# The front of an attention block in a written-out order: who evicts a tile's first group, when two query weights are loaded, and in which pieces two heads' second halves are computed

## The chip, the cores and the metric

One Trainium2 chip; the same program runs on 8 cores at once, each on its own 1024 rows (own rows), without talk between the cores. The metric is the device time of the slowest core in microseconds (us), lower is better. Engines: TensorE (PE: matmuls, transposes), VectorE (DVE), ScalarE (ACT), GpSimd (POOL), and SyncE (SP), which issues loads. Each engine works through its own list of instructions in order; where an instruction waits for a semaphore, all that stands behind it on the engine waits too.

## The reference, cut to what matters

x is (2, 4096, 4096) in float32. Two layers: `x = x + LN(attn(LN(x)))`, then `x = x + LN(ffn(LN(x)))`.

```python
Q = (x @ Wq.T).reshape(B, S, 32, 128)        # 32 heads
K = x @ Wk.T; V = x @ Wv.T                   # one head of 128, shared
Qr = Q*cos + rotate_half(Q)*sin; Kr likewise # "rope"
# windows of 512 keys every 256 rows: sigmoid(scores*SCALE), each row divided by
# its sum, then @ V; neighbouring windows are blended linearly
return out @ Wo.T
# ffn: x @ base_W.T + 2 * (gates of the top 2 of 8 experts * (x@A_e)) @ B_e
```

## The kernel before, in words

Each core holds 12 tiles of 128 rows: 8 own tiles and 4 neighbour tiles (halo), of which only K and V are needed. `ORDER` gives the order of loading: positions 0 to 7 are the own tiles, 8 to 11 the halo tiles. The part that changes is the front, up to about 185 us, where x becomes K, V and the first queries. After it come 128 steps of attention (with the other heads' queries between the steps), the Wo projection, the second layer norm with transposes and router, and the base projection.

What happens to a tile i in the front:

- `load_x(i)` on SP: three DMAs (2048, 1024, 1024 columns, 2 MB in all) into one of three buffers `xst`, once tile i-3 is normalised.
- `ln1_stats(i)` on VectorE: eight `bn_stats` (L260), then the aggregate and two small instructions.
- `ln1_apply(i)` on ScalarE: three small instructions, then two activations that write the normalised bf16 tile `xn` by halves (L278).
- `ln1_tr(i, g)` on TensorE, g = 0 to 3: eight 128x128 transposes each (L300) into one PSUM bank. There are three banks, `T1_BANK = [0, 1, 7]`, and group 3 takes group 0's: it waits until group 0 is evicted. Groups 0 and 1 need the first half of `xn`, 2 and 3 the second.
- eviction into `ln1T` (or `halo`): groups 0 to 2 on ScalarE (L309), group 3 on VectorE (`ln1_ev3`, L319).
- `kv_mm(i, 0, 32)` on TensorE: 32 matmuls of 256 columns (L329), after all four evictions. `k_rope(i)` on VectorE (L343 to L348), `k_tr(i)` on TensorE (L353, L355) with a copy on ScalarE (L358).

Queries: a job is half a head, 512 rows wide: 32 matmuls in 8 groups of 4 (`q_group`, L406), into bank 4 or 5. Jobs run (0,0), (1,0), (0,1), (1,1), then (2,0), (2,1), (3,0), (3,1), as (head, half). Half 0 needs tiles 0 to 3, half 1 tiles 4 to 7. `ropes()` queues the rope of each finished job on VectorE: four instructions (L418 to L424), of which the first three read the bank. A head's 1 MB weight (2 MB in DRAM, cast by the DMA) comes by `load_wq` on POOL's queue; heads 0 and 1 use slots 2 and 3, and heads 2 and 3 use the same two after them.

The order: in `start_stage(i)`, TensorE gets groups 0 to 2 of tile i-1, K and V of tile i-2, and group 3 of tile i-1. VectorE gets the eviction of group 3, `k_rope(i-2)` and the statistics of tile i+1. ScalarE gets the evictions and `ln1_apply(i)`. Then come `k_tr(i-3)` and, from stage 4 on, four query groups (eight from stage 8), and ropes from stage 7. Weight 0 is loaded once tile 3's first part has landed, cos and sin after tile 4, weight 1 after tile 5's first part.

In the later stage (about 1206 to 1311 us) a loop over 8 tiles computes slab 0 of the base projection. Ahead of the next tile's transposes (`tr_group`, L874), which wait for VectorE's `st_d` (L862), an `early` call puts eight matmuls of slab 1 as filler at t = 2, 3, 4 and 5. Their weights, pieces 38 and 39, are loaded at t = 0 by POOL's queue, behind its own addition `st_add` (L847).

Of the kernel before, what the change touches and what calls it, by code (L numbers as in the profile page):

```python
# [9 lines left out]
BF16 = mybir.dt.bfloat16  # L10
# [10 lines left out]
NTX = 12  # L21
# [66 lines left out]
def tok(s):  # L88
    return (s, s.n)


def build_program():
# [156 lines left out]
    def load_kcs(i):  # L249
        buf, ext = i % 4, ORDER[i]  # L250
        P.op("sync", lambda e: e.dma_start(out=kcs_s[buf][:, :], in_=kcs[ext * 128:(ext + 1) * 128, :]),
             waits=([krp_tok[i - 4]] if i >= 4 else []), inc=s_kcs[buf], inc_by=16)
        kcs_tok[i] = tok(s_kcs[buf])

    ln1_in = {}

    def ln1_stats(i):
        buf, q = i % 3, i & 1
        for k in range(8):
            P.op("vector", lambda e, k=k: e.bn_stats(st[:, q, k, :], xst[buf][:, 512 * k:512 * (k + 1)]),  # L260
                 waits=([x_part[i][{0: 0, 4: 1, 6: 2}[k]]] if k in (0, 4, 6) else []), inc=(s_f if k == 7 else None))
        P.op("vector", lambda e: e.bn_aggr(mv[q], st[:, q, :, :]),
             waits=[tok(s_f)] + ([xap_tok[i - 2]] if i >= 2 else []), inc=s_f)
        P.op("vector", lambda e: e.tensor_scalar(lnv[q], mv[q][:, 1:2], EPS, None, ALU.add),
             waits=[tok(s_f)], inc=s_f)
        P.op("vector", lambda e: e.tensor_scalar(mv[q][:, 0:1], mv[q][:, 0:1], -1.0, None, ALU.mult), inc=s_f)
        ln1_in[i] = tok(s_f)
# [27 lines left out]
    def ln1_tr(i, g):  # L295
        q, bk = i & 1, g % 3
        pb = ps[T1_BANK[bk]].bitcast(BF16)
        for k in range(8):
            dt = 8 * g + k
            P.op("tensor", lambda e, k=k, dt=dt: e.transpose(  # L300
                    pb[:, k * 128:(k + 1) * 128], xn[q][:, dt * 128:(dt + 1) * 128], identB[:, :]),
                 waits=([xap_half[(i, g // 2)], ID_READY] + t1_free[bk]) if k == 0 else [],
                 inc=(s_t1 if k == 7 else None))
        t1_tok[i] = [tok(s_t1)]
        src = pb.rearrange("p (a b) -> p a b", a=8)
        dst = ln1_view(i)(8 * g, 8 * g + 8)
        halo_free = [kv_tok[i - 2]] if ORDER[i] in (10, 11) and g == 0 else []
        if g < 3:
            P.op("scalar", lambda e: e.activation(out=dst, in_=src, func=AF.Copy),  # L309
                 waits=[tok(s_t1)] + halo_free, inc=s_t1a)  # L310
            t1_free[bk] = [tok(s_t1a)]
            ev_tok.setdefault(i, []).append(tok(s_t1a))

    def ln1_ev3(i):
        pb = ps[T1_BANK[0]].bitcast(BF16)
        src = pb.rearrange("p (a b) -> p a b", a=8)
        dst = ln1_view(i)(24, 32)
        halo_free = [kv_tok[i - 2]] if ORDER[i] in (10, 11) else []
        P.op("vector", lambda e: e.tensor_copy(dst, src), waits=t1_tok[i] + halo_free, inc=s_t1v)  # L319
        t1_free[0] = [tok(s_t1v)]  # L320
        ev_tok[i].append(tok(s_t1v))

    kvb_free = [[], []]

    def kv_mm(i, d0, d1):
        bk = i & 1
        view = ln1_view(i)
        for d in range(d0, d1):
            P.op("tensor", lambda e, d=d: e.matmul(  # L329
                    ps[2 + bk][:, 0:256], view(d, d + 1), wkv_s[:, d, :], start=(d == 0), stop=(d == 31)),  # L330
                 waits=((ev_tok[i] + kvb_free[bk]) if d == 0 else [])
                 + ([WKV_READY[d // 8]] if i == 0 and d % 8 == 0 else []),
                 inc=(s_kv if d == 31 else None))
        if d1 == 32:
            kv_tok[i] = tok(s_kv)
# [132 lines left out]
    load_kcs(0)  # L468
    load_kcs(1)

    def start_stage(i):

        if i >= 1 and i - 1 < NTX:
            for g in range(3):
                ln1_tr(i - 1, g)
        if i >= 2:
            kv_mm(i - 2, 0, 32)
        if i >= 1 and i - 1 < NTX:
            ln1_tr(i - 1, 3)
            ln1_ev3(i - 1)  # L480
        if i >= 2:
            k_rope(i - 2)
            if i + 2 < NTX:
                load_kcs(i + 2)
        if i + 1 < NTX:
            ln1_stats(i + 1)
        if i < NTX:
            ln1_apply(i)
            if i + 3 < NTX:
                load_x(i + 3)  # L490
            if i < 2:
                load_kcs(i + 2)
        if i == 1:
            load_wq(0, [x_part[3][0]])
            P.op("gpsimd", lambda e: e.dma_start(out=cosT_s[:, :], in_=cosT[:, :]),
                 waits=[x_part[4][2]], inc=s_cs, inc_by=16)
            P.op("gpsimd", lambda e: e.dma_start(out=sinS_s[:, :], in_=sinS[:, :]), inc=s_cs, inc_by=16)
            cs_ready.append(tok(s_cs))
        if i == 3:
            load_wq(1, [x_part[5][0]])  # L500
        if i == NTX:
            load_wq(4, t1_tok[NTX - 1])
            load_wq(5, t1_tok[NTX - 1])

    ln1_stats(0)
    Q_AHEAD = 64
    for i in range(NTX + 2):
        start_stage(i)
        if i >= 3 and i - 3 < NTX:
            k_tr(i - 3)  # L510
        if i == NTX:
            use_table(AF.Sigmoid)
        if i >= 4:
            for _ in range(4 if i < 8 else 8):
                if q_pos[0] < Q_AHEAD:
                    q_next()
            if i >= 7:
                ropes()
    for h in wq_late:
        load_wq(h, [wq_done[h - 4]])  # L520
    k_tr(NTX - 1)
    while q_pos[0] < Q_AHEAD:
        q_next()
    ropes()
    KR_READY = tok(s_kev)
    KV_DONE = tok(s_kv)
    V_READY = tok(s_vcp)
# [476 lines left out]
    for t in range(NT):  # L1004
        router_mm(t)
        if t + 1 < NT:
            st_d(t + 1)
        router_chain(t)
        if t + 3 < NT:
            st_n(t + 3)  # L1010
            st_add(t + 3, "gpsimd")
            if t + 5 < NT:
                load_xr(t + 5)
        b = t & 1
        breg = ps[b][:, 0:512]
        proj_mms(breg, ln2T, t, BA_P[0], 0, 16, bank_free[b] + [t2_tok[t]], t == NT - 1, t == 0, False)
        if t == 0:
            w7(16, 32)
            w7_done()
            load_piece(38)  # L1020
            load_piece(39)
        elif 2 <= t < 6:
            early((t - 2) // 2, 16 + 8 * ((t - 2) % 2))
        if t + 1 < NT:
            tr_group(t + 1, 0)
            tr_group(t + 1, 1)
        proj_mms(breg, ln2T, t, BA_P[0], 16, 24, [], t == NT - 1, t == 0, False)
# [181 lines left out]
```

How the kernel before makes its waits and increments, by code:

```python
                    def body(eng):  # L76
                        for fn, waits, inc, inc_by in oplist:
                            for s, v in waits:
                                if v > 0:
                                    eng.wait_ge(s.h, v)
                            inst = fn(eng)
                            if inc is not None:
                                inst.then_inc(inc.h, inc_by)
```

## Time and profile before

| | us |
|---|---|
| three timed runs | 1740.9, 1743.73, 1717.39; median 1740.9 |
| the profiled execution | 1722.67 |
| its span on the slowest core (4) | 1721.1 |
| spans, cores 0 to 7 | 1713.3, 1717.1, 1718.1, 1715.8, 1721.1, 1718.3, 1721.1, 1717.4 |
| granted clock, all cores | 0.986 to 0.991 of full speed |
| TensorE busy, core 4 | 1635.1 (95%) |
| VectorE, ScalarE busy, core 4 | 681.9, 559.1 |

The page is of core 4, the slowest. Busy is the time in which an engine has an instruction at work; a row of the timeline merges neighbouring instructions of one kind, and the bracket gives idle time before it and what ended that. TensorE's matmuls overlap, so the distance from start to start tells a group's cost better than its length.

### The profile page before, as it was taken

Reading aid. Unit: us, or ns where it says so; the run is one execution under the profiler, and the core shown is the slowest. Engines: PE = TensorE matmul, PEld = TensorE weight load, DVE = VectorE, ACT = ScalarE, POOL = GpSimd, SP = SyncE. Lnnn points to the kernel's source line nnn. Section 1 sums busy time; section 2 is a strip of 40 time slices with the busy share of each in tenths; the row PEclk is TensorE's granted clock in tenths of the full one; section 3 lists DMA queues with packets and bytes.
Section 4 is the critical chain, followed back from the end, with each engine's and each line's share of the span. In section 5 each row is a group of like instructions: output and inputs, shape, how many; then the busy total and the mean of one; then the engine's idle time right before and its main releaser. Section 6 shows DMA issues by size and latency. Waiting matters only on the chain.

```text
span 1721.1 us, 29291 instructions; the slowest of 8 cores (1713.3 to 1721.1 us)
## 1 busy us (share of the span) xinstructions
PE 1635.1 (95%) x10425; PEld 933.0 (54%) x10600; DVE 681.9 (40%) x1715; ACT 559.1 (32%) x906; POOL 147.1 (9%) x180
## 2 busy tenths in 40 slices
PE   2779999999999999999999999999899999999996
PEld 2556566666666666654444444458555444444763
DVE  4575466665666666661000100003882011000065
ACT  3755344554544554451000000011442000000154
POOL 0000000000000000000000000002650000000010
PEclk8899999999999999999999999999999999999998
DMA  9972624666666632227663356533746425642689
GB/s 232 272 248 55 113 50 74 99 99 99 106 105 109 112 63 50 50 53 127 98 98 61 53 83 98 83 93 121 228 146 112 73 50 88 101 68 51 133 250 288
DMA packets 33852, 193.37 MB, mean 112 GB/s; under 512 B 4528, under 2 KB 7216, under 8 KB 17200
## 3 DMA queue, kind: packets, MB, share of 16 engines
q0 software_dynamic: 20752, 139.57, 45.2%
q1 hardware_dynamic: 12672, 51.91, 9.3%
q8 instruction: 89, 1.46, 0.4%
q14 instruction: 51, 0.42, 0.1%
q10 hardware_dynamic: 288, 0.01, 0.0%
HBM read 279.66 MB, written 41.94 MB: 187 GB/s over the span
## 4 chain that ended last, share of the span: by engine, by line
PE 89%; DMA 5%; DVE 2%; issue 2%; ACT 1%; POOL 0%; SPq 0%; DVEq 0%; ACTq 0%; POOLq 0%
PE ps_all L712 49%; PE ps_all L406 25%; PE ps_all L570 5%; PE ps_all L547 5%; DMA xst<-x_ext 4%; PE ps_all L329 2%; DMA wslot<-wb_scratch 1%; PE ps_all L616 1%; PE ps_all L936 1%; PE ps_all L300 1%; PE ps_all L890 1%; PE ps_all L874 1%; DVE st L260 0%; POOL proj L847 0%; DVE st L729 0%
## 5 line engine op out<-in xcount | busy, mean ns | idle before, releaser
L406 PE MATMUL ps_all<-ln1T,wslot 128*128 128x512 bf16 x1960 | 453.0, 381 | 12.9 <-DVE ln1T L319 8.4
L712 PE MATMUL ps_all<-wslot,ln2T 128*128 128x512 bf16 (+1 forms) x2256 | 452.2, 356 | 5.7 <-DMA wslot<-wb_scratch 3.2
L712 PE MATMUL ps_all<-wslot,attn_T 128*128 128x512 bf16 (+1 forms) x2266 | 441.7, 355 | 2.6 <-ACT attn_T L621 0.6
L729 DVE BATCH_NORM_STATS2 st<-proj 128x6 f32<-128x512 bf16 x192 | 126.4, 687 | 659.6 <-ACT proj L721 659.6
L712 PEld LDWEIGHTS ps_all<-wslot,attn_T 128*128 128x128 bf16 x2304 | 224.8, 98 | 217.0 <-issue 0.8
L712 PEld LDWEIGHTS ps_all<-wslot,ln2T 128*128 128x128 bf16 x2304 | 224.2, 98 | 216.2 <-issue 4.3
L406 PEld LDWEIGHTS ps_all<-ln1T,wslot 128*128 128x128 bf16 x2048 | 200.2, 98 | 223.5 <-issue 11.7
L721 ACT ACTIVATE proj<-ps_all 128x512 bf16<-128x512 f32 (+1 forms) x144 | 78.5, 548 | 680.8 <-PE ps_all L712 378.5
L556 ACT ACTIVATE sig<-ps_all 128x1536 bf16<-128x1536 f32 x128 | 185.6, 1450 | 3.7 <-PE ps_all L547 3.7
L621 ACT ACTIVATE attn_T<-ps_all 128x256 bf16<-128x256 bf16 x128 | 49.1, 383 | 230.2 <-PE ps_all L616 230.2
L570 PEld LDWEIGHTS ps_all<-v_aug,sig 128*128 128x128 bf16 x1536 | 99.5, 98 | 36.8 <-issue 9.5
L570 PE MATMUL ps_all<-v_aug,sig 128*128 128x129 bf16 (+1 forms) x1536 | 113.1, 221 | 3.1 <-DVE cbl L604 2.1
L600 DVE SCALAR_TENSOR_TENSOR ct<-ps_all,urs,ct 128x128 f32<-128x128 f32 x256 | 88.8, 347 | 48.1 <-ACT ct L595 47.6
L604 DVE SCALAR_TENSOR_TENSOR cbl<-ps_all,urs,ct 128x128 bf16<-128x128 f32 x256 | 89.9, 351 | 45.0 <-DVE ct L600 44.6
L547 PE MATMUL ps_all<-qrT,krT 128*128 128x256 bf16 x768 | 104.6, 272 | 0.5 <-ACT krT L358 0.5
L595 ACT ACTIVATE ct<-ps_all,urs 128x128 f32<-128x128 f32 x256 | 80.1, 363 | 65.5 <-DVE urs L587 56.3
L677 POOL DMA_DIRECT2D wslot<-wall x56 | 29.5, 528 | 689.4 <-PE ps_all L712 580.0
L260 DVE BATCH_NORM_STATS2 st<-xst 128x6 f32<-128x512 f32 x96 | 59.5, 682 | 38.9 <-DMA xst<-x_ext 38.9
L547 PEld LDWEIGHTS ps_all<-qrT,krT 128*128 128x128 bf16 x768 | 68.8, 97 | 7.3 <-issue 0.7
L370 POOL DMA_DIRECT2D wslot<-wqp x32 | 17.3, 541 | 615.2 <-PE ps_all L406 551.2
L300 PE MATMUL ps_all<-identB,xn 128*128 128x128 bf16 x384 | 30.9, 242 | 38.4 <-ACT xn L278 37.3
L586 DVE RECIPROCAL urs<-ps_all 128x4 f32<-128x4 f32 x128 | 23.0, 180 | 89.5 <-PE ps_all L570 89.5
(83 smaller groups left out, 884.2 us busy)
## 6 DMA issues: line engine op xcount, KB each, us to landing
wslot<-wall POOLq DMA_DIRECT2D x56, 1024.0 KB, 16.3
wslot<-wqp POOLq DMA_DIRECT2D x32, 1024.0 KB, 11.4
xst<-x_ext SPq DMA_DIRECT2D x12, 1024.0 KB, 18.0
xst<-x_ext SPq DMA_DIRECT2D x24, 512.0 KB, 21.7
out<-oprj SPq DMA_DIRECT2D x22, 512.0 KB, 11.9
xb_scratch<-x_ext POOLq DMA_DIRECT2D x8, 1024.0 KB, 16.6
wb_scratch<-wall POOLq DMA_DIRECT2D x8, 1024.0 KB, 16.5
wslot<-wb_scratch POOLq DMA_DIRECT2D x8, 1024.0 KB, 9.9
```

The lines of the kernel that those rows point to most:

```text
L260: P.op("vector", lambda e, k=k: e.bn_stats(st[:, q, k, :], xst[buf][:, 512 * k:512 * (k + 1)]), waits=([x_part[i][{0: 0, 4: 1, 6: 2}[k]]] ...
L406: P.op("tensor", lambda e, d=d: e.matmul(reg, wt[:, d * 128:(d + 1) * 128], ln1T[:, d, 512 * hf:512 * (hf + 1)], start=(d == 0), stop=(d = ...
L547: P.op("tensor", lambda e, j=j: e.matmul(ps[j // 2][:, (j % 2) * 256:(j % 2) * 256 + 256], krT[:, 256 * c + 128 * j:256 * c + 128 * j + 12 ...
L556: P.op("scalar", lambda e: e.activation(out=sig[b][:, :], in_=ps_all[:, 0:1536], func=AF.Sigmoid, scale=SCALE), waits=[s_tok[k]] + sg_free ...
L570: P.op("tensor", lambda e, j=j, qh=qh, o0=o0, o1=o1, v0=v0, v1=v1: e.matmul(ps[6 + qh][:, o0:o1], sig[b][:, j * 256 + qh * 128:j * 256 + q ...
L595: P.op("scalar", lambda e, i=i, qh=qh: e.activation(out=ct1[i][:, :], in_=ps[6 + qh][:, 0:128], func=AF.Copy, scale=urs[:, o + 4 + 2 * qh: ...
L600: P.op("vector", lambda e, i=i, qh=qh: e.scalar_tensor_tensor(ct2[i][:, :], ps[6 + qh][:, 129:257], urs[:, o + 8 + qh:o + 9 + qh], ct1[i][ ...
L604: P.op("vector", lambda e, i=i, qh=qh: e.scalar_tensor_tensor(cbl[i][:, :], ps[6 + qh][:, 258:386], urs[:, o + 5 + 2 * qh:o + 6 + 2 * qh], ...
L621: P.op("scalar", lambda e: e.activation(out=attn_T[:, h, 256 * c:256 * c + 256], in_=at_pb[:, 0:256], func=AF.Copy), waits=[tok(s_at)], in ...
L712: P.op("tensor", lambda e, rhs=rhs, d=d: e.matmul(reg, lhsT[:, d, t * 128:(t + 1) * 128], rhs, start=(d == first), stop=(end and d == 31)) ...
L721: P.op("scalar", lambda e: e.activation(out=dst, in_=reg, func=AF.Copy), waits=[tok(s_grp)], inc=s_gev)
L729: P.op("vector", lambda e: e.bn_stats(st[:, t, k, :], src), waits=waits, inc=s_lnd)
```

## The change

1. `ln1_stats` is cut into `ln1_stats_a` (first four `bn_stats`) and `ln1_stats_b` (the rest and the small ones).
2. VectorE evicts group 0 instead of group 3, ScalarE groups 1 to 3. All four transposes of a tile now stand together, ahead of K and V, with the next tile's statistics around the eviction.
3. The order of the front is written out by hand; two more query groups stand between a late tile's transposes and its K and V.
4. Weight 0 is loaded behind tile 3's second part, and weight 1, cos and sin right behind it in POOL's queue.
5. The second halves of heads 0 and 1 are computed by pairs of tiles (`q_pair`, 256 columns at a time): tiles 4 and 5, then 6 and 7.
6. In the later stage, `early` moves from t = 2..5 to t = 3..6.

```diff
-        if g < 3:
+        if g == 0:
+            P.op("vector", lambda e: e.tensor_copy(dst, src), waits=[tok(s_t1)] + halo_free, inc=s_t1v)
+            t1_free[bk] = [tok(s_t1v)]
+            ev_tok[i] = [tok(s_t1v)]
+        else:
             P.op("scalar", lambda e: e.activation(out=dst, in_=src, func=AF.Copy),
                  waits=[tok(s_t1)] + halo_free, inc=s_t1a)
-    def ln1_ev3(i):
...
+    def q_pair(h, p, u0, u1):
+        reg = ps[4 + h][:, 256 * (p - 2):256 * (p - 1)]
+        wt = wslot[wq_slot(h)]
+        for d in range(4 * u0, 4 * u1):
+            ws = []
+            if d == 0:
+                ws = (qb_free[h] if p == 2 else []) + ev_tok[2 * p] + ev_tok[2 * p + 1]
...
+        if p == 3 and u1 == 8:
+            wq_done[h] = tok(s_q)
+            pending.append((h, 1, h, tok(s_q)))
+            load_wq(h + 2, [wq_done[h]])
...
+    def t_step(i):
+        late = i in (1, 3, 4)
+        if i + 1 < NTX and not late:
+            ln1_stats_a(i + 1)
+        for g in range(4):
+            ln1_tr(i, g)
+        if i + 1 < NTX:
+            if late:
+                ln1_stats_a(i + 1)
+            ln1_stats_b(i + 1)
+            ln1_apply(i + 1)
+            if i + 4 < NTX:
+                load_x(i + 4)
+    def kv(i):
+        kv_mm(i, 0, 32)
+        k_rope(i)
+        if i + 4 < NTX:
+            load_kcs(i + 4)
...
+    load_wq(0, [x_part[3][1]])
+    t_step(0)
+    load_wq(1, [])
...
+    t_step(4)
+    k_tr(3)
+    kv(4)
+    qs(6)
+    t_step(5)
+    k_tr(4)
+    qs(2)
+    ropes()
+    kv(5)
+    q_pair(0, 2, 0, 8)
+    q_pair(1, 2, 0, 6)
+    t_step(6)
+    k_tr(5)
+    q_pair(1, 2, 6, 7)
+    kv(6)
+    t_step(7)
+    k_tr(6)
+    q_pair(1, 2, 7, 8)
+    kv(7)
+    q_pair(0, 3, 0, 8)
+    q_pair(1, 3, 0, 6)
+    t_step(8)
+    k_tr(7)
+    q_pair(1, 3, 6, 8)
+    kv(8)
+    ropes()
+    q_pos[0] = 32
+    for i in range(9, NTX):
+        t_step(i)
+        k_tr(i - 1)
+        qs(2)
+        kv(i)
+        qs(8)
+        ropes()
...
-        elif 2 <= t < 6:
-            early((t - 2) // 2, 16 + 8 * ((t - 2) % 2))
+        elif 3 <= t < 7:
+            early((t - 3) // 2, 16 + 8 * ((t - 3) % 2))
```

The last job, (3,1), ends with two groups behind `k_tr(11)`; weights 4 and 5 and the sigmoid table are queued after the loop.

## Rows read from the trace of the kernel before

**Rows 1.** Windows view: length, busy PE, PEld, DVE, ACT, POOL, clock, DMA share, GB/s.
```profile
0.00:185.00 185.00, 133.00 (x1042) 92.27 (x1053) 100.05 (x222) 95.79 (x112) 8.19 (x19) 0.93 0.77 198
185.00:1200.00 1015.00, 1005.19 (x6453) 569.93 (x6567) 415.11 (x1200) 341.48 (x587) 47.45 (x84) 1.00 0.50 87
```

**Rows 2.** Windows view of the front, finer: clock, DMA share and GB/s last.
```profile
40.00:60.00 20.00, 14.92 (x127) 11.93 (x128) 12.33 (x30) 15.30 (x17) 0.54 (x1) 0.74 1.00 260
60.00:80.00 20.00, 15.31 (x120) 10.08 (x119) 11.57 (x29) 10.89 (x14) 1.58 (x3) 0.91 1.01 288
80.00:95.00 15.00, 9.21 (x81) 6.55 (x82) 9.18 (x20) 7.71 (x10) 0.00 (x0) 1.00 0.98 302
95.00:125.00 30.00, 24.84 (x193) 17.22 (x196) 21.75 (x49) 17.30 (x21) 0.13 (x1) 0.89 0.73 249
```

**Rows 3.** Timeline of TensorE: start, length, line, operation, idle before and releaser.
```profile
65.42 4.51 PE L406 MATMUL ps_all<-ln1T,wslot 128*128 128x512 bf16 x15 [3.41 <-DVE ln1T L319]
...
95.06 2.96 PE L300 MATMUL ps_all<-identB,xn 128*128 128x128 bf16 x24 [4.81 <-ACT xn L278]
...
106.94 3.66 PE L329 MATMUL ps_all<-wkv_s,ln1T 128*128 128x256 bf16 x32
110.43 0.61 PE L300 MATMUL ps_all<-identB,xn 128*128 128x128 bf16 x8
...
116.12 8.21 PE L406 MATMUL ps_all<-ln1T,wslot 128*128 128x512 bf16 x31 [4.96 <-DVE ln1T L319]
...
129.77 6.85 PE L406 MATMUL ps_all<-ln1T,wslot 128*128 128x512 bf16 x31
...
148.76 1.50 PE L300 MATMUL ps_all<-identB,xn 128*128 128x128 bf16 x24
...
184.66 0.81 PE L547 MATMUL ps_all<-qrT,krT 128*128 128x256 bf16 x6 [0.52 <-ACT krT L358]
```

**Rows 4.** Timeline of VectorE over the front, same columns.
```profile
88.02 2.57 DVE L260 BATCH_NORM_STATS2 st<-xst 128x6 f32<-128x512 f32 x4 [0.52 <-DMA xst<-x_ext]
...
103.95 4.83 DVE L260 BATCH_NORM_STATS2 st<-xst 128x6 f32<-128x512 f32 x8
...
109.64 0.69 DVE L418 TENSOR_TENSOR qm<-ps_all,cosT_s 128x512 bf16<-128x512 f32 x1
...
112.37 0.69 DVE L418 TENSOR_TENSOR qm<-ps_all,cosT_s 128x512 bf16<-128x512 f32 x1
...
114.91 0.68 DVE L319 COPY ln1T<-ps_all 128x1024 bf16<-128x1024 bf16 x1
115.51 0.28 DVE L343 TENSOR_TENSOR km<-ps_all,kcs 128x128 bf16<-128x128 f32 x1
...
116.16 4.83 DVE L260 BATCH_NORM_STATS2 st<-xst 128x6 f32<-128x512 f32 x8
```

**Rows 5.** Timeline of ScalarE: tile 5 normalised, its neighbour's groups evicted.
```profile
77.60 4.08 ACT L278 ACTIVATE xn<-xst,small 128x2048 bf16<-128x2048 f32 x2
...
81.74 2.83 ACT L309 ACTIVATE ln1T<-ps_all 128x1024 bf16<-128x1024 bf16 x3
```

**Rows 6.** DMA queues from 72 to 77 us: packets, MB, share of 16 engines.
```profile
q0 software_dynamic: 135, 0.64, 61.5%
q1 hardware_dynamic: 132, 0.60, 40.0%
```

**Rows 7.** DMA issues from 124 to 126 us: count, size, us to landing.
```profile
wslot<-wqp POOLq DMA_DIRECT2D x1, 1024.0 KB, 9.4
```

**Rows 8.** Timeline of TensorE around tile 2 of the later stage.
```profile
1244.07 2.45 PE L712 MATMUL ps_all<-wslot,ln2T 128*128 128x512 bf16 x8 [3.16 <-DMA wslot<-wb_scratch]
```

**Rows 9.** Timeline of VectorE in the later stage.
```profile
1227.37 2.02 DVE L862 TENSOR_SCALAR proj<-proj,small 128x4096 bf16<-128x4096 bf16 x1 [0.18 <-DVE small L756]
...
1240.56 2.02 DVE L862 TENSOR_SCALAR proj<-proj,small 128x4096 bf16<-128x4096 bf16 x1 [0.18 <-DVE small L756]
```

**Rows 10.** Waits of TensorE, core 7, 1200 to 1300 us: total, times, longest.
```profile
PE ps_all L874 <- DVE proj L862: 1.4, 5, 0.4
```

More of the change, by code:

```diff
@@ L255, in build_program, with ln1_stats_a, ln1_stats_b @@
     ln1_in = {}
-    def ln1_stats(i):
+    def ln1_stats_a(i):
         buf, q = i % 3, i & 1
-        for k in range(8):
+        for k in range(4):
             P.op("vector", lambda e, k=k: e.bn_stats(st[:, q, k, :], xst[buf][:, 512 * k:512 * (k + 1)]),
-                 waits=([x_part[i][{0: 0, 4: 1, 6: 2}[k]]] if k in (0, 4, 6) else []), inc=(s_f if k == 7 else None))
+                 waits=([x_part[i][0]] if k == 0 else []))
+    def ln1_stats_b(i):
+        buf, q = i % 3, i & 1
+        for k in range(4, 8):
+            P.op("vector", lambda e, k=k: e.bn_stats(st[:, q, k, :], xst[buf][:, 512 * k:512 * (k + 1)]),
+                 waits=([x_part[i][k // 2 - 1]] if k in (4, 6) else []), inc=(s_f if k == 7 else None))
         P.op("vector", lambda e: e.bn_aggr(mv[q], st[:, q, :, :]),
@@ L306, in ln1_tr @@
         dst = ln1_view(i)(8 * g, 8 * g + 8)
-        halo_free = [kv_tok[i - 2]] if ORDER[i] in (10, 11) and g == 0 else []
-        if g < 3:
+        halo_free = [kv_tok[i - 2]] if ORDER[i] in (10, 11) and g < 2 else []
+        if g == 0:
[3 more added lines that the diff above has]
+        else:
             P.op("scalar", lambda e: e.activation(out=dst, in_=src, func=AF.Copy),
@@ L311, in ln1_tr @@
             t1_free[bk] = [tok(s_t1a)]
-            ev_tok.setdefault(i, []).append(tok(s_t1a))
-    def ln1_ev3(i):
[L315 to L321, printed above, removed]
+            ev_tok[i].append(tok(s_t1a))
     kvb_free = [[], []]
@@ L429, in build_program @@
     cs_ready = []
+    def q_pair(h, p, u0, u1):
[5 more added lines that the diff above has]
+                ws = (qb_free[h] if p == 2 else []) + ev_tok[2 * p] + ev_tok[2 * p + 1]
+            P.op("tensor", lambda e, d=d: e.matmul(
+                    reg, wt[:, d * 128:(d + 1) * 128], ln1T[:, d, 256 * p:256 * (p + 1)],
+                    start=(d == 0), stop=(d == 31)),
+                 waits=ws, inc=(s_q if d == 31 else None))
+        if p == 3 and u1 == 8:
+            wq_done[h] = tok(s_q)
+            pending.append((h, 1, h, tok(s_q)))
+            load_wq(h + 2, [wq_done[h]])
     q_pos = [0]
@@ L469, in build_program @@
     load_kcs(1)
[L471 to L484, printed above, removed]
-        if i + 1 < NTX:
[L486 to L503, printed above, removed]
@@ L505, in build_program @@
-    ln1_stats(0)
-    Q_AHEAD = 64
[L507 to L518, printed above, removed]
+    def t_step(i):
[4 more added lines that the diff above has]
+            ln1_tr(i, g)
+        if i + 1 < NTX:
+            if late:
[4 more added lines that the diff above has]
+                load_x(i + 4)
@@ new lines, in kv, with qs @@
+    def kv(i):
[3 more added lines that the diff above has]
+            load_kcs(i + 4)
+    def qs(n):
+        for _ in range(n):
+            q_next()
+    ln1_stats_a(0)
+    ln1_stats_b(0)
+    ln1_apply(0)
+    load_x(3)
+    load_kcs(2)
+    load_kcs(3)
+    load_wq(0, [x_part[3][1]])
+    t_step(0)
+    load_wq(1, [])
+    P.op("gpsimd", lambda e: e.dma_start(out=cosT_s[:, :], in_=cosT[:, :]), inc=s_cs, inc_by=16)
+    P.op("gpsimd", lambda e: e.dma_start(out=sinS_s[:, :], in_=sinS[:, :]), inc=s_cs, inc_by=16)
@@ new lines, in build_program @@
+    cs_ready.append(tok(s_cs))
+    t_step(1)
+    kv(0)
+    t_step(2)
+    kv(1)
+    k_tr(0)
+    t_step(3)
+    kv(2)
+    k_tr(1)
+    kv(3)
+    qs(8)
+    k_tr(2)
+    t_step(4)
[19 more added lines that the diff above has]
+    q_pair(1, 3, 0, 6)
@@ L519, in build_program @@
+    t_step(8)
[4 more added lines that the diff above has]
+    q_pos[0] = 32
+    Q_AHEAD = 64
+    for i in range(9, NTX):
[3 more added lines that the diff above has]
+        kv(i)
+        qs(8)
+        ropes()
+    load_wq(4, t1_tok[NTX - 1])
+    load_wq(5, t1_tok[NTX - 1])
+    use_table(AF.Sigmoid)
+    k_tr(NTX - 1)
+    qs(2)
+    ropes()
     for h in wq_late:
         load_wq(h, [wq_done[h - 4]])
-    k_tr(NTX - 1)
-    while q_pos[0] < Q_AHEAD:
-        q_next()
@@ L524, in build_program @@
-    ropes()
     KR_READY = tok(s_kev)
```

## The prediction

> **What bounds the kernel now.** I read the windows first. From 185 to 1200 us TensorE is busy 1005.2 of 1015 us at full clock: nothing in that stretch can be won by order. In the first 185 us it is busy 133.0 us, at a mean clock of 0.93 [rows 1]. So the front holds what can be won, and a little lies in the later stage. The finer windows say why TensorE waits: from 40 to 95 us the DMA engines are full (shares 1.00, 1.01, 0.98); after 95 us they fall to 0.73 [rows 2]. Up to there the arrival of x sets the pace; after that the order does. In TensorE's timeline the reader should see three stops of over 3 us with slow work behind them: 3.41 us before 65.42, 4.81 before 95.06, 4.96 before 116.12 [rows 3]. The last ends by VectorE's eviction of tile 7's group 3, queued behind two ropes (109.64 to 114.91 us) [rows 4]. From 116.12 TensorE runs without a gap that matters to the first scores at 184.66.
>
> **Unit costs.** Start to start: K and V of a tile 3.49 us (106.94 to 110.43), so 0.109 us per 256-column matmul. 24 transposes show 1.50 us and 8 show 0.61, so 16 cost 0.89 and a tile's 32 cost 1.78. 31 matmuls of 512 columns show 6.85 us: 0.216 each, a group of four 0.86 [rows 3]. On VectorE: four statistics 2.42 us (half of 4.83), a rope 2.7, an eviction 0.6 to 0.7, `k_rope` 0.65 (115.51 to 116.16) [rows 4]. On ScalarE: normalising 4.08 us, an eviction 0.94 [rows 5]. From the last statistics of a tile (88.02+2.57=90.6) to its first transposes (95.06) are 4.4 us [rows 3, 4], to its second half 2 us more [rows 5].
>
> **Part by part.** *Pairs of tiles.* 128 matmuls of 256 columns replace 64 of 512: 14.0 us against 13.8. The rows of K and V have the same shape, so I take +0.1 us. What it buys: 15 of these 32 groups can run before tile 7 is there.
>
> *Loads.* The x tiles and both weights, cos and sin must all land by tile 6, before and after; with the DMA full to 95 us [rows 2], moving the weights forward moves tile 5 back and leaves tile 6 at its 89 us. I cost it at nothing; the cover is that POOL's transfers are through by then. The first rope needs cos and sin at 91 us, fine.
> When POOL's queue and SP's were both at work they took 61.5% and 40.0% [rows 6]. The Trainium skill (DMA: Bandwidth & Descriptors, Queues, rings and completion order) says that each DMA engine goes round the queues that have work, a packet at a time; by that rule four transfers standing together on POOL's queue hold x to the smaller share for longer. The row agrees; it is the slow rival below.
>
> *Eviction of group 0 on VectorE.* Now a tile's four groups stand together, and group 3 needs group 0's bank. With VectorE free this is cheap: group 0 done after 0.6, evicted 0.7 later, so 0.2 us of stop. ScalarE's third eviction ends at about tile start + 4.05 us, and K and V can't start before: where `k_tr` and two query groups (1.73+0.1) stand between, 0.2 us is lost; where less stands there (tiles 7 and 8), 0.65 and 1.05. But where VectorE is not free, all of TensorE stands behind group 3:
> - Tile 9: `kv(8)`, then both ropes of the second halves, then `ln1_stats_a(10)`, then the eviction. From the end of K and V of tile 8: 0.65+2×2.65+2.42+0.7=9.1 us, against 1.3 us of transposes that TensorE still has. Idle 7.8 us, in two pieces around the second half's arrival.
> - Tile 10: the rope of (2,0) starts six groups into `qs(8)`: 2.7+2.4+0.7=5.8 us against 1.73+1.34. Idle 2.8 us.
> - Tile 11: no statistics behind, and its rope is ready four groups earlier: 0.2.
>
> *The clock.* After the 4.96 us stop the same 31 matmuls take 8.21 us instead of 6.85, and after the 4.81 us stop 24 transposes take 2.96 instead of 1.50 [rows 3]: 1.4 us each. The 7.8 us stop will cost 1.4 too, the 2.8 us one between 0 and 1.1 (the stop of 3.41 us was followed by 15 matmuls in 4.51 us). I take 1.4 in all.
> The Trainium skill (TensorE: Matmul & The Clock Gate, Part 4) holds that transposes don't bring the clock up. The row shows transposes at 56 ns each when matmuls ran before; by that page group 3 behind the long stop would stay slow, which is 0.4 us, no more.
>
> *When tile 7 starts.* Tile 6's last part is in at 89.3, statistics to 90.6, the small ones to 91.4. VectorE then has two ropes to 96.7, `k_rope(5)` to 97.3, four statistics of tile 7 to 99.7. TensorE: tile 5's group 3 waits for the eviction behind four statistics of tile 6, which start when that lands (85.0): 88.3. Then two query groups, K and V of tile 5 to 94.2, 14 units of pairs (6.1) to 100.3. Tile 6 starts there, its group 0 is evicted at 101.7, the rest of tile 7's statistics ends at 104.1. Tile 7 starts at 104.1+4.4=108.5; before, it started at 105.6.
>
> *From there to the first scores.* Work: five tiles' transposes 8.9, five times K and V 17.45, one and 16 units of pairs 7.4, 32 groups 27.6, `k_tr` 0.7: 62.1 us. Stops: tile 7's second half and group 3 1.8, its K and V 0.65; tile 8 0.2 and 1.05; tile 9 its start 0.7 and 7.8; tile 10 2.85; tile 11 0.3: 15.3. Clock 1.4. Sum 78.8: scores at 187.3, against 184.66 [rows 3]: **+2.6 us**. The gain in work done early (62.1 left instead of about 74) is spent on VectorE's order.
>
> *Weights 2 to 5.* Weight 2 is issued when (0,1) ends, wanted 10.8 us of work plus the 7.8 us stop later; it landed in 9.4 us [rows 7]. Weight 4 waits for tile 11's transposes, now 14 us before the attention, against 19: covered by the same 9.4. Nothing; without cover 1 or 2 us.
>
> *Later stage.* On core 4 the filler at t = 2 waited 3.16 us for its weights and then ran slow, 2.45 us [rows 8]; the transposes behind it began at 1246.3. Without it they wait for VectorE only: 1240.56+2.02=1242.6 [rows 9]: 3.7 us earlier. The eight matmuls (1.73 us) come back at t = 6, where VectorE leaves them no hole: **-1.9 us**. VectorE's period per tile is 13.19 us (1227.37 to 1240.56) [rows 9]; on core 7, without the weight's stop, TensorE waits for VectorE at five tiles (1.4 us) [rows 10], so that core gains nothing at t = 2 and pays +1.7 at t = 6. Its span was 1717.4, so it comes to 1719.1, level with core 4's 1719.2.
>
> **Sum.** 1722.67+2.6-1.9=1723.4, say **1723**, of the profiled execution. The runs shown have the median 1740.9, and one of three at 1717.39: an unchanged kernel gives either. I forecast by the profile and let the range reach their upper end. Two per cent is 34 us, about what a measurement of this kernel tells from no change; the front's whole stops are not much more.
>
> **Rivals.**
> (a) *Tile 6 lands earlier.* Weight 1 no longer stands beside it (before it landed at 84.3, together with tile 6's first part at 85.0). If that frees it, up to 5.5 us earlier, the whole of TensorE's and VectorE's chain follows: 1717 to 1718. Against: the DMA was full, so somebody else has to land later; nothing useful stands behind but tile 5, which had slack. Chance 0.25.
> (b) *VectorE's queue is no bar.* The written order is then worth what it looks like: all stops but the small ones (7.8+2.85+1.4 clock) fall away, 1711; with tile 7 earlier too, 1706. Against: a VectorE queue is in order, and the ropes stand ahead of the eviction in the text. The reason to keep it: K and V of tile 8 may end before VectorE gets there only in part. Chance 0.1.
> (c) *Slower: the loads' share.* With 61.5% to POOL's queue from 47 us on, tile 5 comes at 80 instead of 76 and tile 6 behind it late as well; from 2 us on nothing hides it, since tile 6's landing heads the chain to tile 7. Five us late: 1728; with the 2.8 us stop's clock in full, 1730. Chance 0.2.
> (d) *The change doesn't do what it says*: the stop at the filler stays (weights land still later, as the front shifts all) and the front as forecast: 1725; no piece of mine tells it from the forecast. Inside the forecast.
> Forecast 0.45.
>
> **Range.** The cases reach from 1706 to 1730 on the execution's own scale. The timed runs spread from 1717 to 1744 for one kernel, so the range is 1706 to 1744. Within 2% 0.97; faster by more 0.01 (it would take the sum of all front stops), slower by more 0.02.
>
> **What would show it.** In the changed profile: tile 7's transposes near 108; group 3 of tile 9 waiting for VectorE's L319 copy, 5 to 8 us, at 133 to 140, with slow matmuls behind; a second such stop of 3 us 15 us later; first scores at 185 to 189; no stop by wb_scratch at t = 2, TensorE waiting there for VectorE instead. Wrong would be: tile 6 in at 84 or 94 instead of 89, or the stops before tiles 9 and 10 gone.

## The result and the profile after

The changed kernel took 1751.8 us (median of 5; 1748.8 to 1993.4) against 1719.9 us (median of 5 of the kernel before), ratio 1.0161 [1.0104, 1.0219]. The forecast was 1723, "within 2%", with a range to 1744. It is outside the range, and slower.

That ratio can't be read without one fact: in each of those five executions two to four cores ran part of the way at a lower granted clock, which comes to the kernel before too (1740.9 and 1743.7 among its five), so like must be put beside like. The view of spans and mean clocks of the profiled execution shows it on cores 0 and 1:

```profile
core 0: 1744.2 us, clock 0.974
core 1: 1747.5 us, clock 0.971
core 2: 1729.1 us, clock 0.989
core 3: 1729.1 us, clock 0.988
core 4: 1727.5 us, clock 0.986
core 5: 1728.8 us, clock 0.987
core 6: 1727.6 us, clock 0.989
core 7: 1730.1 us, clock 0.985
```

The windows of core 1, then of core 4 (length, busy PE, PEld, DVE, ACT, POOL, then clock, DMA share, GB/s):

```profile
60.00:110.00 50.00, 48.03 (x341) 33.11 (x340) 25.25 (x59) 21.28 (x26) 0.00 (x0) 0.79 0.80 235
...
210.00:260.00 50.00, 50.00 (x353) 29.63 (x352) 27.42 (x83) 22.93 (x37) 1.59 (x3) 0.98 0.50 87
```

```profile
60.00:110.00 50.00, 43.77 (x359) 31.77 (x358) 29.16 (x67) 25.45 (x32) 0.00 (x0) 0.93 0.81 252
...
210.00:260.00 50.00, 50.00 (x371) 30.33 (x370) 31.54 (x97) 25.71 (x44) 1.59 (x3) 1.00 0.36 64
```

Core 1 is granted 0.79 of the full 2.4 GHz from 60 to 110 us with TensorE busy 48 of 50 us, where core 4 has 0.93; from 210 us on both are near full. The 32 matmuls of K and V of tile 5 take 4.36 us on core 1 and 3.65 on core 4. The low clock is 20 us of span (1747.5 against 1727.5), and nothing shows it to be the change's: the same kernel run again later took 1732.1 to 1734.6 us in five of six executions, ratio 1.0076 [1.0062, 1.009], **+13 us**. This is what has to be explained.

TensorE's timeline on core 4 (a core near full clock, as the slowest one before was):

```profile
74.59 2.67 PE L306 MATMUL ps_all<-identB,xn 128*128 128x128 bf16 x32
...
78.85 5.39 PE L330 MATMUL ps_all<-wkv_s,ln1T 128*128 128x256 bf16 x32 [1.37 <-ACT ln1T L319]
84.08 5.34 PE L407 MATMUL ps_all<-ln1T,wslot 128*128 128x512 bf16 x24
89.25 2.16 PE L306 MATMUL ps_all<-identB,xn 128*128 128x128 bf16 x32
...
103.12 2.16 PE L306 MATMUL ps_all<-identB,xn 128*128 128x128 bf16 x32
...
111.44 1.05 PE L306 MATMUL ps_all<-identB,xn 128*128 128x128 bf16 x16 [0.41 <-ACT xn L284]
...
130.99 3.65 PE L330 MATMUL ps_all<-wkv_s,halo 128*128 128x256 bf16 x32 [1.11 <-ACT halo L319]
...
144.01 1.01 PE L306 MATMUL ps_all<-identB,xn 128*128 128x128 bf16 x8 [6.47 <-DVE halo L315]
...
145.03 3.01 PE L407 MATMUL ps_all<-ln1T,wslot 128*128 128x512 bf16 x8
147.88 3.66 PE L330 MATMUL ps_all<-wkv_s,halo 128*128 128x256 bf16 x32
...
162.71 0.61 PE L306 MATMUL ps_all<-identB,xn 128*128 128x128 bf16 x8 [2.92 <-DVE halo L315]
...
163.26 1.89 PE L407 MATMUL ps_all<-ln1T,wslot 128*128 128x512 bf16 x8
...
191.94 0.82 PE L602 MATMUL ps_all<-qrT,krT 128*128 128x256 bf16 x6
```

The reader is to see four things. Tile 4's transposes start at 74.6 and tile 7's at 111.4, where tile 7's started at 105.6 before. Group 3 of tile 9 waits 6.47 us for VectorE's eviction (L315), group 3 of tile 10 another 2.92; before, the long waits for VectorE's eviction were 3.41 and 4.96 us [rows 3]. After the long stop 8 matmuls take 3.01 us where 8 take 1.89 at full clock (163.26). And the first scores come at 191.9 against 184.7.

VectorE's timeline of the same core, the small aggregates (L268) of tiles 4, 5 and 7, the two halves of tile 6's statistics (L260, L266), then what is queued behind K and V of tile 8:

```profile
68.05 0.37 DVE L268 BATCH_NORM_AGGREGATE small<-st 128x2 f32<-128x48 f32 x1 [0.17 <-DVE st L266]
...
80.92 0.37 DVE L268 BATCH_NORM_AGGREGATE small<-st 128x2 f32<-128x48 f32 x1 [0.17 <-DVE st L266]
...
85.15 2.46 DVE L260 BATCH_NORM_STATS2 st<-xst 128x6 f32<-128x512 f32 x4
89.97 0.69 DVE L315 COPY ln1T<-ps_all 128x1024 bf16<-128x1024 bf16 x1 [2.36 <-PE ps_all L306]
90.58 2.46 DVE L266 BATCH_NORM_STATS2 st<-xst 128x6 f32<-128x512 f32 x4
...
107.08 0.37 DVE L268 BATCH_NORM_AGGREGATE small<-st 128x2 f32<-128x48 f32 x1 [0.17 <-DVE st L266]
...
134.88 0.29 DVE L344 TENSOR_TENSOR km<-ps_all,kcs 128x128 bf16<-128x128 f32 x1 [3.50 <-PE ps_all L330]
...
135.55 0.68 DVE L419 TENSOR_TENSOR qm<-ps_all,cosT_s 128x512 bf16<-128x512 f32 x1
...
138.27 0.69 DVE L419 TENSOR_TENSOR qm<-ps_all,cosT_s 128x512 bf16<-128x512 f32 x1
...
140.81 2.46 DVE L260 BATCH_NORM_STATS2 st<-xst 128x6 f32<-128x512 f32 x4
143.19 0.67 DVE L315 COPY halo<-ps_all 128x1024 bf16<-128x1024 bf16 x1
```

The queue is in the order in which it was written: `k_rope` at 134.9, two ropes, four statistics at 140.8, and only then the eviction at 143.2, for which TensorE has waited since 137.5.

Stage by stage, from the timelines of all eight cores (means in us; cores at the low clock are left out; the end of the statistics is the start of the tile's aggregate):

| | before | changed | changed, again |
|---|---|---|---|
| tile 7's statistics end | 96.1 | 106.8 | 106.3 |
| first scores | 183.5 | 193.6 | 192.8 |
| first scores to end of Wo part | 1021.7 | 1021.1 | 1021.1 |
| stage with the filler | 103.1 (102.3 to 105.3) | 103.9 | 104.0 |
| rest | 409.4 | 410.1 | 411.5 |

So the front costs 9 to 10 us against this profile, and the filler 0.8 on the mean, 1.6 on a core that had no stop for its weights. Two of the experiments below keep the old order of the front and have their first scores at 180.8 and 182.5, so the front's loss is 9 to 13 us, known no closer than that. The rest adds 1 to 2 us on the mean; it differs by 2 to 10 us from core to core in every kernel, and no part of the change touches it. In place of the 3.16 us stop for wb_scratch [rows 8] stands this wait, in total, times and longest, core 4, changed kernel:

```profile
PE ps_all L929 <- DVE proj L917: 2.6, 3, 2.0
```

### The profile page after: what moved, and what is told of

It reads as the page before. It is cut to its first block, busy times and chain, and to the rows that moved or that the text cites. A ratio compares the mean times of both kernels' runs of the same rounds, so it can differ in the third digit from the quotient of the medians.

```text
span 1747.5 us, 29606 instructions; the slowest of 8 cores (1727.5 to 1747.5 us)
## 1 busy us (share of the span) xinstructions
PE 1667.6 (95%) x10664; PEld 950.0 (54%) x10664; DVE 682.5 (39%) x1715; ACT 561.9 (32%) x906; POOL 146.5 (8%) x180
## 4 chain that ended last, share of the span: by engine, by line
PE 91%; DVE 3%; DMA 2%; issue 2%; ACT 1%; SPq 0%; DVEq 0%; ACTq 0%
PE ps_all L767 49%; PE ps_all L407 25%; PE ps_all L625 5%; PE ps_all L602 5%; PE ps_all L330 3%; DMA xst<-x_ext 2%; DVE st L784 1%; PE ps_all L440 1%; PE ps_all L671 1%; PE ps_all L306 1%; PE ps_all L991 1%; PE ps_all L945 1%; PE ps_all L929 1%; DVE st L260 0%; ACT xn L284 0%
## 5 line engine op out<-in xcount | busy, mean ns | idle before, releaser
L407 PE MATMUL ps_all<-ln1T,wslot 128*128 128x512 bf16 x1984 | 461.9, 386 | 0.5 <-issue 0.5
L407 PEld LDWEIGHTS ps_all<-ln1T,wslot 128*128 128x128 bf16 x1984 | 196.7, 99 | 214.2 <-issue 29.7
L655 DVE SCALAR_TENSOR_TENSOR ct<-ps_all,urs,ct 128x128 f32<-128x128 f32 x256 | 88.6, 346 | 48.4 <-ACT ct L650 48.0
L650 ACT ACTIVATE ct<-ps_all,urs 128x128 f32<-128x128 f32 x256 | 80.5, 365 | 65.1 <-DVE urs L642 56.1
L306 PEld LDWEIGHTS ps_all<-identB,xn 128*128 128x128 bf16 x384 | 30.2, 118 | 51.3 <-issue 50.8
## 6 DMA issues: line engine op xcount, KB each, us to landing
xst<-x_ext SPq DMA_DIRECT2D x24, 512.0 KB, 16.8
```

Source lines behind the costliest of these rows:

```text
L306: P.op("tensor", lambda e, k=k, dt=dt: e.transpose(pb[:, k * 128:(k + 1) * 128], xn[q][:, dt * 128:(dt + 1) * 128], identB[:, :]), waits=( ...
L407: P.op("tensor", lambda e, d=d: e.matmul(reg, wt[:, d * 128:(d + 1) * 128], ln1T[:, d, 512 * hf:512 * (hf + 1)], start=(d == 0), stop=(d = ...
L650: P.op("scalar", lambda e, i=i, qh=qh: e.activation(out=ct1[i][:, :], in_=ps[6 + qh][:, 0:128], func=AF.Copy, scale=urs[:, o + 4 + 2 * qh: ...
L655: P.op("vector", lambda e, i=i, qh=qh: e.scalar_tensor_tensor(ct2[i][:, :], ps[6 + qh][:, 129:257], urs[:, o + 8 + qh:o + 9 + qh], ct1[i][ ...
```

## The experiments

First scores are given as the mean over the cores near full clock: 183.5 before (180.8 in e1, which has the same front), 193 for the changed kernel. Ratios are against the kernel before on the same chip in the same session.

### The filler alone, and the front alone

```diff
# e1: the kernel before with
-        elif 2 <= t < 6:
-            early((t - 2) // 2, 16 + 8 * ((t - 2) % 2))
+        elif 3 <= t < 7:
+            early((t - 3) // 2, 16 + 8 * ((t - 3) % 2))
# e2: the changed kernel with the reverse of this
```

> The kernel before with the later stage's part alone (the filler at t = 3..6). Order theory: TensorE's 3.2 us stop for wb_scratch at t = 2 goes, a wait of about 2 us for VectorE takes its place, the filler is paid at t = 6: core 4 -1.4, core 7 +1.5 us, slowest core 0 to -2 us, ratio 0.999 to 1.000. Clock theory (the changed front brings on the lower granted clock of two to four cores, 0.81 from about 58 to 212 us): this kernel has the old front, so its executions are no more often at 1740 and above than those of the kernel before. Chance theory: the low clock in a pair of cores comes as often here as anywhere, two of five.

Measured: ratio 1.0019 [1.0005, 1.0033]. The stage took 104.0 to 104.2 us on every core, against 102.3 on cores before that had no stop for their weights and 105.3 on core 4. The order theory had the two prices about right and missed the ratio: most cores pay. In this profile cores 4 and 5 are the slowest by their last part, 415 us behind the stage against 406 to 412 elsewhere, and not by a stop in it.

> The changed kernel with the filler back at t = 2..5: the front's part alone. Order theory: on cores at the full clock +7 to +9 us against before, first scores near 192 on core 4. Clock theory: two to four cores show a mean clock of 0.97 in at least four of five executions, 1748 to 1752 us. Chance theory: this is seen in about two of five, and the others lie at 1727 to 1733 us.

Measured: ratio 1.0083 [1.0062, 1.0104], four of seven executions at 1732 to 1736, more than the 7 to 9 us that were expected. First scores are at 193.4 (195.2 on core 4). The stage took 102.3 to 102.4 us on all eight cores, although five of them stopped 0.5 to 1.4 us for wb_scratch at the filler: stops of that length do not lengthen the stage. The front's part alone makes nearly the whole loss. By the stage's length the old place of the filler is 1.5 us better; the timed ratios, 1.0083 here and 1.0076 for the whole change in another session, are too close to show it. That a changed front brings on the low clock isn't borne out: none of the seven lies at 1748 to 1752.

### The four statistics behind the eviction

```diff
-        late = i in (1, 3, 4)
+        late = i in (1, 3, 4, 9, 10)
```

> The changed kernel with the first four statistics of tiles 10 and 11 behind the eviction of group 0 instead of ahead of it. Order theory: TensorE's stop before group 3 of tile 9 goes from 6.5 to 4.1 us and that of tile 10 from 2.9 to 0.5: 4.8 us less on cores at full clock, first scores near 187. Rival (the stop is the normalised tile's or a bank's): no change. On the clock no theory expects a change: if executions come down by 20 us, the long stop brought on the low clock.

Measured: ratio 1.0057 [1.0041, 1.0073]; first scores at 187.8, 5.6 us earlier than in e2. TensorE's timeline, core 4, tile 9's group 3:

```profile
141.72 1.01 PE L306 MATMUL ps_all<-identB,xn 128*128 128x128 bf16 x8 [4.11 <-DVE halo L315]
```

The stop is 4.11 us (4.1 was expected) and tile 10's is 0.55. Each went down by 2.4 us, the length of the four statistics moved behind the copy: there, what stood in VectorE's queue set TensorE's time one for one. The two together are 4.7 of the 5.6 us by which the front came earlier.

### The ropes ahead of K and V of tile 8

```diff
+    ropes()
     t_step(8)
     k_tr(7)
     q_pair(1, 3, 6, 8)
+    ropes()
     kv(8)
-    ropes()
# and: late = i in (1, 3, 4, 8, 9, 10); the filler back at t = 2..5
```

> The changed kernel with the two ropes of the second halves queued ahead of K and V of tile 8 instead of behind it, the first four statistics of tiles 9 to 11 behind the eviction, and the filler back at t = 2..5. Order theory: the stop of tile 9's group 3, 6.5 us in the changed kernel and 4.1 with the statistics alone moved, goes to under 1, with the slow matmuls behind it; first scores at 181 to 184, the later stage at 102.4 instead of 103.9 us; ratio to before 0.998 to 1.003. Rival (the late start of tile 7 alone makes the loss): first scores no lower than 187, ratio 1.005.

Measured: ratio 1.0028 [1.0006, 1.0049]; eight executions with all cores near full clock took 1721.8 to 1725.8 us, sixteen of the kernel before 1719.5 to 1723.6. First scores are at 183.9 on the six cores near full clock. The stops of tiles 9 and 10 on core 4:

```profile
136.74 1.05 PE L306 MATMUL ps_all<-identB,xn 128*128 128x128 bf16 x16 [2.69 <-ACT xn L284]
...
155.56 0.61 PE L306 MATMUL ps_all<-identB,xn 128*128 128x128 bf16 x8 [0.55 <-DVE halo L315]
```

Nothing waits for VectorE's copy at tile 9 any more; TensorE waits 2.69 us for the normalised tile instead, whose statistics end at 132.5 and not 130.7, behind the rope. At tile 10 0.55 us are left of 2.92. Together with the statistics this recovers 9 us of the front. Tile 7's statistics still end at 105.8, ten us later than before, so the rival falls: a late tile 7 costs little by itself once VectorE's queue is out of the way. On core 3 a stop of 1.55 us for weight 2 appeared as well; the long stop had stood between its issue and its use.

### All four groups on ScalarE

```diff
-        if g == 0:
-            P.op("vector", lambda e: e.tensor_copy(dst, src), waits=[tok(s_t1)] + halo_free, inc=s_t1v)
-            t1_free[bk] = [tok(s_t1v)]
-            ev_tok[i] = [tok(s_t1v)]
-        else:
-            (the "scalar" branch, for g = 1 to 3)
+        (the "scalar" branch, for all g)
```

> The changed kernel with all four groups of a tile evicted on ScalarE. Order theory: TensorE never waits for VectorE's eviction (6.5, 2.9 and 1.2 us go, with 1.4 us of slow clock), and the statistics no longer wait for tile i's transposes, so that those of tile 7 end before 105; in exchange K and V of a tile start 0.9 us later at each of some eight tiles. Sum -3 to -8 us, first scores 186 to 190. Rival (ScalarE with 4 evictions and the normalising becomes the bound, 9 us of the tile's 14): first scores stay at 193 or later.

Measured: ratio 1.0056 [1.0017, 1.0095], which counts three executions at 1743 us that have two to four cores at a mean clock of 0.97. The five with all cores near full clock took 1723 to 1726 us, 3 us above the kernel before and some 9 below the changed one; first scores at 186.5. Two waits of TensorE on core 4:

```profile
107.52 3.65 PE L325 MATMUL ps_all<-wkv_s,ln1T 128*128 128x256 bf16 x32 [1.70 <-ACT ln1T L314]
...
140.43 3.00 PE L402 MATMUL ps_all<-ln1T,wslot 128*128 128x512 bf16 x7 [3.11 <-DVE qm L417]
```

No eviction waits for VectorE, and tile 7's statistics end at 103 instead of 107. In exchange K and V wait 1.7 us for ScalarE at tiles 6 and 7, 1.3 at tile 8, and (2,0) waits 3.11 us for the rope that frees its bank (L417): VectorE's two ropes come back as another wait, smaller than the 6.47 us. Moving the eviction to VectorE was the worse choice in this order.

### The loads as before, in the changed order; the early loads, in the old order

```diff
# e4: the changed kernel
-    load_wq(0, [x_part[3][1]])
+    load_wq(0, [x_part[3][0]])
     t_step(0)
-    load_wq(1, [])
-    P.op("gpsimd", ... cosT_s ...)
+    P.op("gpsimd", ... cosT_s ..., waits=[x_part[4][2]], ...)
...
     t_step(1)
+    load_wq(1, [x_part[5][0]])
# e10: the kernel before with the change's loads
-            load_wq(0, [x_part[3][0]])
+            load_wq(0, [x_part[3][1]])
+            load_wq(1, [])
...
-            load_wq(1, [x_part[5][0]])
# and cos and sin no longer wait for tile 4
```

> The changed kernel with weight 0 behind tile 3's first part, cos and sin behind tile 4, weight 1 behind tile 5's first part, as before. Load theory: tile 4's last part lands at 63 us instead of 66.6, tile 5's transposes start 2 to 4 us earlier, first scores 2 to 4 us earlier than 192 on core 4. Rival: tile 4's landing varies by itself between executions, and tile 6 then lands at 89 as before and holds TensorE back; no gain, or a loss of up to 2 us. If the low clock is brought on by the full DMA queues with dense TensorE work, it gets rarer here.

Measured: ratio 1.0105 [1.008, 1.0129]; first scores at 194.9, 1 to 2 us later than with the early loads. Tile 4's statistics end at 62.5 us (68 with the early loads), as the load theory said; but tile 5's gain only 2 us, tile 6's end at 92.6 to 96.2, and TensorE stops for weight 1 (core 4 below, 4.50 us on core 7):

```profile
83.68 5.12 PE L407 MATMUL ps_all<-ln1T,wslot 128*128 128x512 bf16 x23 [2.10 <-DMA wslot<-wqp]
```

> The kernel before with the change's loads alone: weight 0 behind tile 3's second part, weight 1, cos and sin right behind it. Load theory: tile 4's statistics end at 67 to 69 us instead of 63 to 64, but the DMA engines are full until all of it is in, so tile 6's end at 86 to 91 as before: first scores within 1.5 us of before's (181 to 187), or up to 2 us earlier since weight 1 holds TensorE no more at 85 us. Rival (the 4 us at tile 4 pass through to the end, as they did in the changed order): first scores 3 to 5 us later, ratio 1.002 to 1.003.

Measured: ratio 1.0019 [1.0009, 1.003]; first scores at 182.5. Tile 4's and tile 6's aggregates on core 4:

```profile
66.92 0.37 DVE L262 BATCH_NORM_AGGREGATE small<-st 128x2 f32<-128x48 f32 x1 [0.17 <-DVE st L260]
...
86.22 0.37 DVE L262 BATCH_NORM_AGGREGATE small<-st 128x2 f32<-128x48 f32 x1 [0.17 <-DVE st L260]
```

Tile 4 is 3 us later than before (63.6), and tile 6's statistics end at 86.2, no later than with the old loads (88.6 on the mean before, 86.2 in e1). In the old order the early loads shift tile 4 and cost the front nothing; in the changed order taking them back made the front no earlier. But e4 traded the late tile 4 for a stop at weight 1, so what the late tile 4 costs by itself in that order stays open. The ratio is the one that the rival expected and has no counterpart in the front; its cause stays open.

### Without the pairs of tiles

```diff
-    q_pair(0, 2, 0, 8)
-    q_pair(1, 2, 0, 6)
...
-    q_pair(0, 3, 0, 8)
-    q_pair(1, 3, 0, 6)
+    qs(8)
+    qs(6)
     t_step(8)
     k_tr(7)
-    q_pair(1, 3, 6, 8)
+    qs(2)
```

> The changed kernel without the pairs: the second halves of heads 0 and 1 run at 512 columns after K and V of tile 7. Pair theory: 15 units (6.5 us) of TensorE's work can't run before tile 7; TensorE reaches tile 6 about 6 us earlier and then waits for its data; tile 7 starts 2 to 4 us earlier, and the front ends 3 to 5 us later than the changed kernel's (193): the pairs do earn what was claimed. Rival (VectorE's chain sets tile 7's start and it follows TensorE's order): tile 7's statistics come as much earlier as TensorE reaches tile 6, and the front ends within 1.5 us of 193.

Measured: ratio 1.02 [1.014, 1.0261], of which part is the low clock on two to four cores in five of its six executions; the sixth took 1742.2, 1.012 of the kernel before. First scores are at 200.5 on the six cores near full clock, 7 us later than with the pairs. TensorE came to tile 6 some 5 us earlier, and stopped there for the eviction behind VectorE's ropes (core 4):

```profile
104.23 1.01 PE L306 MATMUL ps_all<-identB,xn 128*128 128x128 bf16 x8 [3.24 <-DVE ln1T L315]
```

The stops of tiles 9 and 10 stand there as in the changed kernel, 6.47 and 2.92 us. The pair theory has the sign right and the size too small: the pairs are worth 7 us in this order, since they also fill the time in which VectorE works off two ropes. Tile 7's statistics came 1 us earlier (105.6 on the mean), neither the 2 to 4 us of the pair theory nor the 5 us by which TensorE reached tile 6.

### The kernel before with its ropes moved

```diff
-            if i >= 7:
+            if i == 6 or i >= 8:
                 ropes()
```

> The kernel before with one condition changed: the rope of (0,0) is queued a stage earlier (stage 6), and that of (1,0) a stage later (behind tile 7's eviction). Order theory: VectorE has no rope ahead of the eviction of tile 7's last group, so TensorE's stop of 4.6 to 5.0 us goes to about 0.9, and the 1.4 us of slow clock behind it too: -4 to -6 us, first scores 177 to 180 where before has 181 to 187, ratio 0.997. Rival (the stop moves to the bank that the rope frees, or to tile 8's data): less than 2 us.

Measured: six of eight executions at 1711.9 to 1718.5 us, against 1719.5 to 1723.6 in sixteen of 25 of the kernel before: 6 us less on the mean, without overlap. The ratio 0.9979 [0.9946, 1.0012] also counts one of 1732.6 us with two cores at a mean clock of 0.97. In the profiled execution, the fastest of the eight, every core's span is 1706.4 to 1710.3. VectorE and TensorE on core 4:

```profile
96.32 0.69 DVE L418 TENSOR_TENSOR qm<-ps_all,cosT_s 128x512 bf16<-128x512 f32 x1 [0.37 <-issue]
...
109.16 0.69 DVE L319 COPY ln1T<-ps_all 128x1024 bf16<-128x1024 bf16 x1 [1.88 <-PE ps_all L300]
...
116.19 0.69 DVE L418 TENSOR_TENSOR qm<-ps_all,cosT_s 128x512 bf16<-128x512 f32 x1
```

```profile
110.22 6.85 PE L406 MATMUL ps_all<-ln1T,wslot 128*128 128x512 bf16 x31 [1.05 <-DVE ln1T L319]
...
177.40 0.81 PE L547 MATMUL ps_all<-qrT,krT 128*128 128x256 bf16 x6 [0.52 <-ACT krT L358]
```

One rope stands at 96.3, in time that VectorE had free; the eviction of tile 7's group 3 at 109.2 has no rope ahead of it, and the two others follow at 116. TensorE's stop is 1.05 us instead of 4.96 [rows 3], the 31 matmuls behind it take 6.85 us and not 8.21, and first scores come at 174.9 on the mean. That is 8.6 us before the 183.5 of the first profile and 6 before the 180.8 of e1, which has the same old front; 4 to 6 us and 177 to 180 were expected. This one condition beats both kernels.

### The changed kernel again

> The changed kernel itself once more, to separate its own cost from the granted clock. Chance theory (the low clock of two to four cores comes to either kernel): most executions lie at 1728 to 1736 us, all cores at 0.98 to 0.99, some at 1748 to 1752; the ratio to before in like clock is 1.006 to 1.010. Clock theory (the changed kernel brings it on): nearly all executions lie at 1748 us or above, as in its first five.

Measured: 1732.1 to 1734.6 in five of six, ratio 1.0076 [1.0062, 1.009]; first scores at 192.8. The chance theory fits better: in that session the kernel before lies at 1743.6 to 1747.8 us in five of 18 executions, and e1, with the old front, lay at 1749.5 to 1751.1 in four of 13; the changed kernel was at 1748.8 to 1752.2 in four of its first five and in none of these six.

## Why the prediction was wrong, point by point

- **What bounds the kernel, unit costs**: right. On the mean nothing from the first scores to the later stage moved by more than 0.6 us.
- **The stops of tiles 9 and 10**: right in place, cause and size. Forecast 7.8 us in two pieces and 2.8; measured 0.87+6.47 and 2.92 on core 4. e3 and e5 show them to be VectorE's queue, the statistics and the ropes each by their own length.
- **When tile 7 starts**: the step that failed first in the front, by 2.9 us (108.5 forecast, 111.4 measured). I let tile 6's landing head the chain: four statistics of it at 85.0, the eviction behind them, group 3 of tile 5 at 88.3. In the changed kernel no statistics of tile 6 wait for a load (85.15 and 90.58 above), and the eviction at 89.97 waits for TensorE, which came to tile 5 only at 89.25, so that group 3 began at about 90.7. What headed the chain was TensorE's own order from tile 4 on: its transposes stood behind tile 4's late landing (statistics done at 68.0 against 63.6), and K and V of tile 4 then took 5.2 us from start to start instead of 3.5, at a granted clock of 0.58 to 0.66 from 75 to 84 us. That slow stretch alone is 1.7 us, and my clock term had nothing ahead of tile 9. On core 3, whose K and V of tile 4 ran at full clock, TensorE was at tile 5 at 87.5. The share of the late landing stays open, as said at e4; e10 shows that the old order swallows it.
- **From there to the first scores**: 78.8 forecast, 80.5 measured. From start to start the stops come to 16.8 us instead of 15.3, a few tenths more at each small one of tiles 7, 8, 10 and 11; the slow matmuls behind the long stop cost 1.6, for which I had 1.4.
- **The front's sum**: +2.6 forecast, +7.3 on the same core, +9 to +10 on the mean of the same profiles. The sign was right. I took core 4 for all; before, its front (184.7) was among the late ones, so it had less to lose than most.
- **The loads at nothing**: not refuted for the front (e4, e10). The pairs at +0.1 us of work were right; what they buy, 7 us (e7), was in the sum only through the work left. Weights 2 to 5 at nothing was right too, by the long stop's cover: e5, without that stop, waits 1.55 us for weight 2 on core 3.
- **The later stage**: the two prices were right (-1.9 and +1.7 forecast, -1.4 on core 4 and +1.6 on core 7), the sum was wrong. I booked core 4's gain because core 4 was the slowest. But core 6 had the same span of 1721.1, and its stage took 103.5 us before against 103.9 now: it gains nothing. Only cores 4 and 5 took longer than 103.9 before. The term should have been near +1.6; e2 gives +1.5.
- **The measured time**: 1723.4 forecast, 1733 of its own (front 4.7 to 7 more than forecast, stage 3.5); the rest to 1751.8 is the low clock, which the forecast had only in its range. The range's upper end took the kernel before's worst runs and added nothing for this kernel's own loss: it should have been 1744 and the loss on top.
- **The rivals**: (a) and (b) did not come. (c), 1728 to 1730, lay nearest in time, but by luck: tile 5's statistics did end at 81, yet its late tile 6 did not head the chain to tile 7. In (b) the queue was every bit the bar that the text makes it.

## What to carry to other kernels

When work is reordered, write down each engine's queue as a list and ask of every short instruction that frees a bank what stands ahead of it: a 0.7 us copy behind two ropes and four statistics cost 6.5 us, and moving one `ropes()` in the old order was worth 6 us of the whole. The written order also tied tile i+1's statistics to tile i's eviction, so that tile 7's ended at 107 instead of 96; whether running them a tile ahead would help was not tried, and e5 won most of the front back without it. And sum a change for every core before naming the slowest; a gain that only one core has is gone as soon as another core leads.

## What the runs showed of the hardware that I had not expected

- Two neighbouring cores (0 and 1, 2 and 3, 4 and 5, or 6 and 7) can be granted about 0.8 of the full clock for 100 to 170 us while others of the same four are at full clock: 60 to 210 us on core 1 of the changed kernel, 150 to 320 us on core 6 without the pairs (granted 0.81 from 200 to 300 us with TensorE busy throughout; first scores to end of the Wo part 1040.9 us against 1021.5). It is neither of the two levels, 1.2 and 2.4 GHz, and no switching between them either: on core 1, 32 matmuls of 256 columns take 4.36 us at 63, 97 and 113 us alike, where 3.65 is the full clock. It costs 16 to 25 us each time. It comes to kernels old and new; what sets it off stays open.
- A late load need not stay late: tile 4's statistics ended 3 to 5.5 us later with the early loads, and tile 6's ended no later than before in the old order (86.3 against 86.2 to 88.6) and 2 us earlier than with the old loads in the changed one (92.9 against 94.8).
- The clock rose after a stretch of transposes alone, where the prediction takes over that transposes don't bring it up. In e5 on core 3 (row below), after an idle time of 2.69 us, TensorE had nothing but the 32 transposes of tile 9 from 138.0 us on. Its granted clock was 0.50 from 138 to 141 us and 0.99 from 141 to 142. The size that the prediction worked out from it did come true: group 3 behind the long stop of tile 9 took 1.01 us instead of 0.61, the 0.4 us of the prediction.

```profile
138.01 3.51 PE L306 MATMUL ps_all<-identB,xn 128*128 128x128 bf16 x32 [2.69 <-ACT xn L284]
```
